# Two attention score triangles packed into one tile, and the router and down weights prepared elsewhere, in a four-layer fp32 kernel on Trainium2

## What is computed

```
# feed-forward: weights are ternary (-s, 0, s)
h1, h3 = x @ q(w1).T, x @ q(w3).T;  y = (silu(h1) * h3) @ q(w2).T

# attention: 16 query heads, 8 key heads of 128, window of 256
mask   = (j <= i) & (i - j < 256)
logits = where(mask, q @ k.T * scale, min)
enc    = softmax(logits) @ v;  y = enc @ out_kernel

# experts
logits = x @ router_weight.T          # 8 experts
gate   = sigmoid(x @ shared_gate_w.T) # 1 row
```

## Time and profile before

| | |
|---|---|
| Median of 3 runs | 2045.21 us (2043.68 to 2047.81) |
| Profiled execution, its own time | 2038.54 us |
| Span in its profile | 2036.6 us |
| PE busy | 1954.8 us (96%) |
| DVE, ACT, POOL busy | 1480.0 us (73%), 1197.9 us (59%), 798.1 us (39%) |
| Recurrence and feed-forward | 0 to about 400 us |
| Attention, PE without a gap | about 470 to 1236 us |
| Last head and norms | to 1356 us |
| Experts | 1358 to 2036.6 us |

### The profile page before, as it was taken

The page is one execution under the profiler, slowest core; times in us unless marked ns, Lnnn a source line. Parts: engine busy times, 40 slices in busy tenths (PEclk is TensorE's granted clock), DMA queues, the critical chain, the costliest instruction groups (busy, mean ns, idle before and its releaser), DMA issues. The chain is left out here.

```text
span 2036.6 us, 32134 instructions
## 1 busy us (share of the span) xinstructions
PE 1954.8 (96%) x10142; PEld 1657.0 (81%) x10142; DVE 1480.0 (73%) x3410; ACT 1197.9 (59%) x2978; POOL 798.1 (39%) x1200
## 2 busy tenths in 40 slices
PE   7999999989999999999999999969999999999996
PEld 5677777768888888888888888858788888888875
DVE  7788565787777777777777778956387778774665
ACT  6752222467666666666666667754376677674342
POOL 4342000685655555555555557942500000001452
PEclk9999999999999999999999999979999999999998
DMA  7343010227000000000000000233799899884563
GB/s 266 124 140 139 16 47 21 84 68 238 22 11 22 11 22 12 9 25 1 22 12 22 32 1 17 61 105 130 257 334 319 310 328 317 310 308 143 198 204 110
DMA packets 82662, 245.28 MB, mean 120 GB/s; under 512 B 10800, under 2 KB 11440, under 8 KB 80592
## 3 DMA queue, kind: packets, MB, share of 16 engines
q1 hardware_dynamic: 77376, 226.46, 32.5%
q0 software_dynamic: 5120, 16.78, 2.3%
HBM read 207.81 MB, written 45.61 MB: 124 GB/s over the span
## 5 line engine op out<-in xcount | busy, mean ns | idle before, releaser
L307 PE MATMUL l_xp<-att_w_hi,xT_hi 128*128 128x512 f32 x512 | 209.8, 410 | 4.8 <-ACT att_qkv L2414 4.3
L307 PE MATMUL l_xp<-att_w_hi,xT_lo 128*128 128x512 f32 x512 | 202.5, 396 | 0.0
L307 PE MATMUL l_xp<-att_w_lo,xT_hi 128*128 128x512 f32 x512 | 202.3, 395 | 0.0
L2443 ACT ACTIVATE att_pr<-att_pr,rec_nb,rec_r 128x384 f32<-128x384 f32 (+2 forms) x256 | 168.6, 662 | 36.3 <-DVE rec_nb L1585 35.6
L946 POOL TENSOR_SCALAR att_pr<-att_pr,rec_ri 128x384 f32<-128x384 f32 (+2 forms) x256 | 140.4, 560 | 124.8 <-DVE rec_ri L1614 121.1
L3874 POOL DMA_INDIRECT y<-moe_rows,moe_slotA x16 | 16.4, 1026 | 414.7 <-DMA moe_rows<-moe_lo_f 411.6
L950 POOL TENSOR_TENSOR att_rot<-att_rot,att_rot 128x384 f32<-128x384 f32 x128 | 129.7, 1014 | 108.9 <-DVE att_rot L1608 108.9
L1581 DVE CUSTOM_DVE_ANT_0 att_pr<-l_dd,att_mask 128x384 f32<-128x384 f32 (+2 forms) x256 | 119.0, 501 | 70.5 <-PE l_dd L307 64.1
L2414 ACT ACTIVATE att_qkv<-l_xp 128x512 f32<-128x512 f32 x128 | 76.3, 596 | 124.9 <-PE l_xp L307 116.4
L1619 DVE TENSOR_TENSOR att_pT_lo<-l_out,att_pT_hi 128x768 fp32r<-128x768 f32 (+2 forms) x128 | 108.7, 849 | 28.9 <-ACT att_pT_hi L2436 28.8
L2436 ACT ACTIVATE att_pT_hi<-l_out 128x768 fp32r<-128x768 f32 (+2 forms) x128 | 92.5, 723 | 41.8 <-PE l_t L307 21.2
(11 more groups left out here) (325 smaller groups left out, 6541.3 us busy)
## 6 DMA issues: line engine op xcount, KB each, us to landing
y<-in_moe_rt SPq DMA_DIRECT2D x59, 704.0 KB, 6.3
y<-in_moe_rt SPq DMA_DIRECT2D x39, 768.0 KB, 6.2
moe_sraw_gu<-in_moe_sgu SPq DMA_DIRECT2D x44, 512.0 KB
moe_sraw_d<-in_moe_sd SPq DMA_DIRECT2D x44, 256.0 KB
moe_xs<-in_zeros SPq DMA_DIRECT2D x39, 256.0 KB, 8.1
...
```

What stands on the lines that cost most here:

```text
L307: mm = pe.matmul(out, lhsT, rhs, start=(i == 0), stop=(i == len(terms) - 1))
L2443: act.activation(p, p, ACT.Exp, scale=r[:, j % 4, g:g + 1], bias=nb_[:, j % 2, g:g + 1], accum_out=sm[:, j % 2, g:g + 1]).then_inc(sa("exp ...
```

## The change

**Scores packed.** In a full step the first key tile counts only above the diagonal and the last only up to it, so both fit into one tile of 128 keys. DVE first copies the last tile over the first one in PSUM wherever key <= token (`copy_predicated`), for both heads at once, and then takes the maximum of both heads in one `reduce_max` over 2 tiles. `exps` reads the scores from PSUM and writes `pr`, so `scores` of the next step now waits for `exp`, not for `mx`. `pr`, `weigh`, `turn_p` and both `split_p` have 2 tiles instead of 3. After the turn the packed tile is parted again: DVE multiplies hi and lo by a triangle (`part_a`, `pA`), and POOL subtracts that from the whole (`part_c`, `pC`). `weigh_v` keeps its 9 matmuls, and waits for `pA` before the 4th and for `pC` before the 7th. `ps_pt` is now used in two halves in turn, and `qkv` and `raw_o` changed places.

**Down weights.** The last group's ternary down weights have a buffer of their own, `wd_last`, and their `tern_d` stands ahead of the products of the group before.

**Router.** The 8 router rows and the gate row ride along in the DMA of `W_dt` at the start of the kernel and are split with it; POOL puts hi and lo side by side (20 columns) into a buffer that lives through all phases. The router then needs 8 matmuls for each block of 512 tokens, not 12, and neither a DMA nor a split; one addition on DVE joins the two halves of the result.

```diff
 def row_max(j, m):                                   # DVE
-    w = ktiles(j) * P
-    wait(dve, "pturn", m - 1)
-    for g in range(GRP):
-        dve.tensor_tensor_reduce(pr[:, j % 2, g, WT * P - w:WT * P], ps_s[:, g, 0:w],
-                                 mask[:, WT * P - w:WT * P], 1.0, -3e38, ALU.add, ALU.max,
-                                 mx[:, j % 2, g:g + 1]).then_inc(sa("mx"), 1)
+    last = ps_s[:, :, P * (w - 1):P * w]
+    if w == WT:
+        dve.copy_predicated(ps_s[:, :, 0:P], mask[:, 0, :].bitcast(mybir.dt.uint32).unsqueeze(1)
+                            .broadcast_to([P, GRP, P]), last).then_inc(sa("mx"), 1)
+    else:
+        dve.tensor_tensor(last, last, mask[:, 2, :].unsqueeze(1).broadcast_to([P, GRP, P]), ALU.add) \
+            .then_inc(sa("mx"), 1)
+    dve.wait_ge(sa("mx"), 2 * m + 1)
+    dve.reduce_max(mx[:, j % 2, :], ps_s[:, :, 0:packed(j) * P], AX.X).then_inc(sa("mx"), 1)
...
+def part_a(j, m):                                    # DVE
+    dve.wait_ge(sa("pT_lo"), m + 1)
+    dve.tensor_tensor(pA[:], pT[:, :, 0, :, :].bitcast(F32), mask[:, 1, :].unsqueeze(1).unsqueeze(1)
+                      .broadcast_to([P, 2, GRP, P]), ALU.mult).then_inc(sa("pA"), 1)
...
+def part_c(j, m):                                    # POOL
+    pool.wait_ge(sa("pA"), full_steps(n) + 1)
+    pool.tensor_tensor(pC[:], pT[:, :, 0, :, :].bitcast(F32), pA[:].bitcast(F32), ALU.subtract)
...
 def exps(j, m):                                      # ACT
+    wait(act, "pturn", m - 1)
     for g in range(GRP):
-        p = pr[:, j % 2, g, WT * P - w:WT * P]
-        act.activation(p, p, ACT.Exp, ...)
+        act.activation(pr[:, j % 2, g, 0:packed(j) * P], ps_s[:, g, 0:packed(j) * P], ACT.Exp, ...)
...
 def scores(j, m):                                    # PE
-    wait(pe, "mx", GRP * m)
+    wait(pe, "exp", GRP * m)
...
 def turn_p(j, m):                                    # PE
-    for u in range(w):
+    for u in range(packed(j)):
...
 def weigh_v(j, m):                                   # PE
+    if w == WT:
+        parts = [(t0 - 1, pT[:, :, 1, :, :], None), (t0 - 2, pA, "pA"), (t0, pC, "pC")]
...
 # DVE, feed-forward to attention
 dve.wait_ge(sa("tab"), 4)
+f.tern_d(dve, FL, CPG, 3 * f.start(FL) + 2 * CPG, (0,))
+f.tern_d(dve, FL, CPG, 3 * f.start(FL) + 2 * CPG, (1,))
+f.tern_d(dve, FL, CPG, 3 * f.start(FL) + 2 * CPG, (2,))
 f.split_lo(dve, FL - 1, NB - 1, CPG - 1)
...
 # PE, experts
-pe.wait_ge(s("rw_lo"), 1)
-    passes(pe, acc[b][:], [(l[:, c, :], r[:, c, bb]) for c in range(KD) for l, r in
-                           ((rw_hi, xT_hi), (rw_hi, xT_lo), (rw_lo, xT_hi))]).then_inc(s("ps_lg"), 1)
+    passes(pe, acc[b][0:2 * NL, :], [(rw_hl[:, c, :], r[:, c, bb]) for c in range(KD) for r in (xT_hi, xT_lo)])
```

1722 lines of the change are left out of this document (905 added, 817 removed).

## The result

The changed kernel is slower: 2058.08 us, median of 4 runs (2056.36 to 2060.45), against 2046.05 us of the kernel before on the same chip (2043.68 to 2047.81, 4 runs); the ratio is 1.006 with a 95% interval of 1.0043 to 1.0078. Its profiled execution took 2057.82 us with a span of 2055.6. The prediction, 2019 us with a range of 2010 to 2037 and 88% on faster, was wrong.

A forecast was written before the change was run, and what follows sets the result against it. PE was taken to bound the middle of the attention (busy 763.8 of 766 us). Turns -18.0, seam -3.0, router -7.9 and ends +3.0 sum to -25.9 us, from 2045.2 to 2019 us; range 2010 to 2037, 80%.

The forecast's parts named there:

- Turns: Middle of the attention: 4 turned tiles instead of 6 save PE 0.22 us in each of 82 full steps, 18.0 us.
- None of them fills the step, so nothing is added in the middle, if the new waits are met.: Middle of the attention: DVE at 81% and POOL at 69% leave room, so their added work costs 0 us.
- The wait of `weigh_v` for `pC`: Attention step: the chain over ACT, DVE and POOL takes about 3.7 us in a gap of 6 us.
- The rule of the shared interface: POOL and DVE contend for SBUF; POOL's rotary sums stayed at 1000 to 1024 ns, so nothing was added.
- The rival that I made of the rule: Last head: part_a holds POOL for 0.68 us, 12 times, 8.2 us on a full engine; 2027 us, 5%.
- the vector engine takes the gain: Middle of the attention: small waits for DVE give back each full step's 0.22 us; 2037 us, 15%.
- score bank: Attention: scores waits for exp at 110 steps, so a late DVE stops PE; slower, 2060 us at 0.5 us a step; 7%.
- Seam: Feed-forward seam: PE's wait falls from 4.4 to about 2.1 us and the clock stays at 1.00; 3.0 us less.
- Router: Start of the experts: PE starts 4.2 us earlier and 16 matmuls drop out, 3.7 us; 7.9 us less.
- Ends: Ends of the attention: DVE and POOL nearly full in the last head, 3 us more; start of the attention 0.

The follow-up runs named there:

- e_rs: Kernel before with the router's and the down weights' parts of the change, its own attention kept: 0.9895 of the kernel before, 0.9924 when run again.
- e_no_ac_o: Changed kernel without part_a and part_c, and with att_o_lo moved behind rope_add(5): 0.986 of the kernel before, middle 654.9 us.
- e_no_ac: Changed kernel without part_a and part_c, the packed tile in their places in weigh_v: 0.9933 of the kernel before, middle 666.2 us.

## Why the prediction was wrong, point by point

The price of the attention in the changed kernel, against `e_rs`, which has all the rest of the change:

| term | forecast us | measured us | from |
|---|---|---|---|
| turns, 72 full steps of the middle | -15.8 | -13.0 | `e_no_ac_o` to `e_rs` |
| `att_o_lo` beside rotary instructions | 0 | +11.3 | `e_no_ac` to `e_no_ac_o` |
| the two products, middle | 0 | +18.0 | changed to `e_no_ac` |
| the two products, last head | +3 for all ends | +11.1 | changed to `e_no_ac` |
| the order, last head (its own saved turns in it) | in the +3 | +5.3 | `e_no_ac` to `e_rs` |

- **Turns.** The step was right: 0.18 us for each full step with 4.2 us of waits left in, 0.24 without them, forecast 0.22.
- **"None of them fills the step, so nothing is added in the middle, if the new waits are met."** This step failed, and with it the forecast. It added up durations per step, left 19% of DVE free, and put the middle's loss at nothing. The two products cost 18.0 us there, with DVE at 87%. The sum itself was low: 29 us more of DVE work between the marks were forecast and 92 came, of which about 55 are instructions that took longer than they need, `part_a` (0.68 taken, 0.84 measured) among them. A step took 684.2/96 = 7.13 us; 6.8 were forecast.
- **The wait of `weigh_v` for `pC`.** ACT, DVE and POOL to `pC` were put at 3.7 us in a gap of 6, so the wait was priced at nothing. In 12 of 72 full steps PE waited for `pC`, 9.6 us in all, since `pA` and then `pC` were held.
- **The rule of the shared interface.** I took the flat 1000 to 1024 ns of POOL's rotary sum as proof that POOL and DVE don't disturb each other. It is flat in the changed kernel as well (mean 1012 ns), where the two plainly do. That sum is released by the last rotary instruction of DVE, so it is the first of the two to start, and the row can't show what it was read for. What is held is mostly DVE, and its rows in the kernel before had it, beside these very sums: 17 `rec_nb` that start while one runs take 0.21 us more in the mean. Below are one of them, and then DVE and POOL at another place, where 0.16, 0.34 and 0.28 us are those instructions' usual times:

```profile
564.44 1.01 POOL L950 TENSOR_TENSOR att_rot<-att_rot,att_rot 128x384 f32<-128x384 f32 x1
564.89 0.59 DVE L1585 SCALAR_TENSOR_TENSOR rec_nb<-rec_mx,rec_r 128x2 f32<-128x2 f32 x1
...
623.06 0.68 DVE L1601 SCALAR_TENSOR_TENSOR att_rot<-att_qkv,rec_r,att_tab 128x128 f32<-128x128 f32 x1
623.66 0.60 DVE L1605 SCALAR_TENSOR_TENSOR att_rot<-att_qkv,rec_r,att_tab 128x64 f32<-128x64 f32 x1
624.18 0.28 DVE L1608 TENSOR_TENSOR att_rot<-att_qkv,att_tab 128x128 f32<-128x128 f32 x1
...
622.95 1.24 POOL L946 TENSOR_SCALAR att_pr<-att_pr,rec_ri 128x384 f32<-128x384 f32 x2 [0.86 <-DVE rec_ri L1614]
```

  The Trainium skill, SBUF — State Buffer, section Who interferes with whom, says that a DVE instruction with two SBUF inputs contends with a GpSimd instruction that reads SBUF, that the port pair they share is an exclusive lock and the order of issue decides who blocks, and that a DVE instruction with at most one SBUF input, outside the 2-port perf modes, does not contend. The traces agree: 2.51 us for 0.28 beside 2.39, 0.84 for 0.16, and 0.69 at most with an operand in PSUM. One row goes against it: POOL's `rec_r` of 128x3 (0.86 us) reads SBUF as well and holds nothing; 30 `rec_nb` that start beside it in the middle of the changed kernel keep 0.16 us. The rival that I made of the rule held POOL alone, with 5% and 2027 us. POOL is held too (`weigh` behind `part_a`), but the larger part is DVE's, and the rival left that out.
- **The order.** I priced each instruction that was added and none that was only moved. The largest single loss, 11.3 us, came from an instruction that the change doesn't touch.
- **Rival "the vector engine takes the gain"** came nearest: PE waits for a late DVE. Its price stopped at giving the gain back, 2037; the median was 2058.
- **Rival "score bank"**: not seen.
- **Seam.** The wait fell from 4.41 to 2.39 us (2.1 forecast) and the clock behind it is 1.00; the part is worth 1 to 3 us on shifted tiles, forecast 3.0. Alone, with the same wait and a clock of 0.50 behind it, it was worth nothing. **Router.** The wait fell by 4.24 us (4.2 forecast); the part is worth 4 to 8 us, forecast 7.9.
- **Ends.** Forecast +3, with 5 as the worse bound and 6 as the sign of being wrong; the last head alone measures +16.4 against `e_rs`. Full engines were counted as full to the brim, without their holding one another; 11.1 of it goes with the two products, and which part of the order costs the rest is open.
- **Luck.** The quicker pitch of the projection, 5 us in the middle, came with the router's 320 bytes and was in no term. Without it the changed kernel would have missed by more.
